# Attention scores of two cross attentions: one bf16 product of 100 rows becomes two float32r products in the row halves of the array

## What is computed

```python
q = split_heads(x @ Wq) / 4            # 2 x 16 heads x 256 x 16
k = split_heads(ctx @ Wk)              # 2 x 16 heads x 4096 x 16
v = split_heads(ctx @ Wv)
scores = einsum('bhqd,bhkd->bhqk', q, k)        # 256 x 4096 for each head
scores = where(mask, -inf, scores)     # layer 1: a large negative number is added
out = einsum('bhqk,bhkd->bhqd', softmax(scores), v)
```

## Time and profile before

| | |
|---|---|
| median of 3 runs | 2161.07 us (2157.18 to 2162.24) |
| profiled execution, span and time | 2163.9 us |
| attention 0, steps under way | about 64 to 519 us |
| attention 1, steps under way | about 760 to 1205 us |
| TensorE busy over the span | 92% |
| VectorE, ScalarE busy | 64%, 52% |

### The profile page before, as it was taken

One profiled execution on the slowest core, in us unless ns is written; L12 is line 12 of the kernel. 1 busy time (PEld: TensorE's weight loads), 2 busy tenths in 40 slices (PEclk: granted clock), 3 DMA queues, 4 the chain that ended last, 5 costly groups with the idle time before them and its releaser, 6 DMA issues.

```text
span 2163.9 us, 36756 instructions
## 1 busy us (share of the span) xinstructions
PE 1995.1 (92%) x13543; PEld 1176.1 (54%) x13543; DVE 1388.0 (64%) x3351; ACT 1131.3 (52%) x2555; POOL 590.4 (27%) x898
## 2 busy tenths in 40 slices
PE   7999999998998799999999888999898799798998
PEld 4545554444465444555445455546646588564656
DVE  4676667785567577666778475442227898577473
ACT  3566666676354366666667461142235587264342
POOL 2322222212542122222220060000015266363241
PEclk9999999999998899999999998999899899999999
DMA  8555445570101655544643201353200333200110
GB/s 192 131 134 123 107 107 136 114 183 15 39 21 40 106 122 133 128 104 106 157 99 60 71 12 35 100 185 98 64 20 2 117 108 93 88 2 8 40 52 10
DMA packets 122835, 187.27 MB, mean 87 GB/s; under 512 B 22920, under 2 KB 70592, under 8 KB 122304
## 3 DMA queue, kind: packets, MB, share of 16 engines
q1 hardware_dynamic: 121568, 183.90, 33.9%
q10 hardware_dynamic: 1088, 1.02, 0.2%
HBM read 131.86 MB, written 2.13 MB: 62 GB/s over the span
## 4 chain that ended last, share of the span: by engine, by line
PE 75%; DVE 12%; ACT 5%; SPq 3%; issue 2%; DMA 2%; POOL 1%; ACTq 0%; DVEq 0%; POOLq 0%
PE PS L759 10%; PE PS L741 10%; PE PS L709 9%; PE PS L340 8%; PE PS L653 5%; PE PS L348 4%; PE PS L665 4%; SPq L781 3%; PE PS L1768 3%; PE PS L1793 3%; PE PS L2201 2%; PE PS L449 2%; PE PS L2143 2%; PE PS L497 2%; PE PS L476 2%
## 5 line engine op out<-in xcount | busy, mean ns | idle before, releaser
L840 DVE TENSOR_REDUCE WK<-PS 128x1 f32<-128x1024 f32 x512 | 609.2, 1220 | 260.8 <-PE PS L709 258.7
L950 ACT ACTIVATE WK<-PS 128x512 f32<-128x512 f32 x1024 | 541.9, 601 | 192.4 <-PE PS L741 186.6
L741 PE MATMUL PS<-WK 100*128 100x256 bf16 x2048 | 323.6, 275 | 6.3 <-ACT WK L950 5.3
L709 PE MATMUL PS<-WK 100*128 100x512 bf16 x1024 | 306.6, 383 | 17.6 <-DMA WK<-scratch_q 5.1
L741 PEld LDWEIGHTS PS<-WK 100*128 100x128 bf16 x2048 | 166.8, 98 | 215.5 <-ACT WK L950 75.2
L759 PE MATMUL PS<-WK 128*32 128x256 f32 x3072 | 207.1, 386 | 0.0
L548 ACT ACTIVATE WK<-PS,WK 128x256 f32<-128x256 f32 (+1 forms) x320 | 140.6, 451 | 74.0 <-DVE WK L516 44.8
L574 POOL TENSOR_TENSOR WK<-WK 128x128 f32<-128x128 f32 (+1 forms) x128 | 64.9, 507 | 342.6 <-DVE WK L534 307.6
L1018 POOL TENSOR_SCALAR WK<-WK 128x2 bf16<-128x2 f32 x64 | 12.5, 195 | 527.5 <-DVE WK L846 329.8
L974 POOL TENSOR_TENSOR WK<-WK 128x512 f32<-128x512 f32 x62 | 71.7, 1157 | 256.9 <-ACT WK L924 147.9
L759 PEld LDWEIGHTS PS<-WK 128*32 128x32 f32 x3072 | 80.6, 109 | 112.4 <-issue 77.6
(11 more groups left out here) (340 smaller groups left out, 3247.7 us busy)
## 6 DMA issues: line engine op xcount, KB each, us to landing
WK<-WK SPq DMA_DIRECT2D x762, 64.0 KB
WB<-in_ctxT SPq DMA_DIRECT2D x78, 512.0 KB, 4.8
WK<-in_ctxT SPq DMA_DIRECT2D x40, 512.0 KB, 3.8
WA<-in_ctxT SPq DMA_DIRECT2D x26, 512.0 KB, 4.8
WK<-in_ctx SPq DMA_DIRECT2D x8, 1024.0 KB, 5.7
WK<-in_ctx SPq DMA_DIRECT2D x16, 512.0 KB, 4.2
WK<-scratch_q SPq DMA_DIRECT2D x24, 128.0 KB, 5.2
WB<-in_L3f_qkv SPq DMA_DIRECT2D x2, 1536.0 KB, 6.5
```

What stands on the lines that cost most here:

```text
L709: x = pe.e.matmul(b.ap[:, u, :], QS[0:100, h, bb * 256 + q * 128:bb * 256 + (q + 1) * 128], KS[s % 4][0:100, c * 1024 + u * 512:c * 1024 + ...
L741: x = pe.e.matmul(b.ap[:, j * 256:j * 256 + 256], KS[s % 4][0:100, kt * 128:(kt + 1) * 128], QS[0:100, h, bb * 256:bb * 256 + 256], start= ...
L840: dv.e.tensor_reduce(mt[:, n:n + 1], tile["R", L, s, n].rearrange("p a b -> p (a b)"), AX, ALU.max).then_inc(*dv.at("R", L, s, n))
L950: ac.e.activation(PR[n % NPR], tile["S", L, s, i], ACT.Exp).then_inc(*ac.at("E", L, s, i))
```

## The change

Instead of three pieces of bf16, a float32 number is split into two pieces of float32r (`FR`, 4 bytes, high and low). A score needs high times high, high times low and low times high: three blocks of 16 rows, two rows for the maxima and one for the mask, 51 rows in all. The two halves of a key tile lie below each other: keys 0 to 2047 on partitions 0 to 50, keys 2048 to 4095 on partitions 64 to 114, and the queries stand on both. `HALF[u]` picks one. A product of the first half uses the upper 64 rows of the array, one of the second the lower 64.

The order is written in **units** `U`, eight to a step: two `S` banks (2 by 2 products, halves alternating), then one `R` pair (one product from each half). `S` order 0 to 15 now alternates between the halves. The projections and `F` stand behind whole units. Before, an `R` stood behind the first `S` of a pair, and at the start of a step ahead of all `S`.

```diff
-        for i in range(16):
-            if i:
-                yield "S", s, i
-            if i % 2 == 0:
-                n = 4 + i // 2 if i < 8 else i // 2 - 4
-                if s + (1 if i < 8 else 2) < 32:
-                    yield "R", s + (1 if i < 8 else 2), n
-            if i == 0:
-                yield "S", s, 0
+        for i in range(0, 16, 2):
+            n = 4 + i // 2 if i < 8 else i // 2 - 4
+            r = s + (1 if i < 8 else 2)
+            row = (r, n) if r < 32 else None
+            yield "U", s, i, row
+            yield "S", s, i
+            if row:
+                yield "R", r, n
+            yield "S", s, i + 1
             if i == 2 and s:
                 if s + 1 < 24:
                     yield "L", s + 1
                 yield "F", s - 1, 3
                 yield "E0", s - 1
-            if i == 5 and 8 <= s < 16:
+            if i == 4 and 8 <= s < 16:
                 yield "V", 1, s - 8, s
             if i in (6, 10, 14):
                 yield "F", s, i // 4 - 1
-            if i == 9 and s < 24:
+            if i == 8 and s < 24:
                 yield "K", s // 4 + 2, s % 4
             if i == 14:
                 yield "M", s + 1
...
+            def row_half(s, n, u):
+
+                g, hh, bb, h = where(s)
+                q, c = n // 4, n % 4
+                return pe.e.matmul(tile["R", L, s, n][:, u, :], QS[HALF[u], g % 2, hh, q * 128:(q + 1) * 128],
+                                   KS[s % 4][HALF[u], c * 512:(c + 1) * 512], start=True, stop=True)
...
+            def column(s, i, j):
+
+                g, hh, bb, h = where(s)
+                kt = i // 2 * 2 + j
+                return pe.e.matmul(tile["S", L, s, i][:, j * 256:j * 256 + 256], KS[s % 4][HALF[i % 2], kt * 128:(kt + 1) * 128],
+                                   QS[HALF[i % 2], g % 2, hh, :], start=True, stop=True)
...
+                elif o[0] == "U":
+                    _, s, i, row = o
                     for u in range(2):
...
+                        column_bank(s, i + u)
+                    for j in range(2):
+                        for u in range(2):
+                            x = column(s, i + u, j)
+                            if j:
+                                x.then_inc(*pe.at("S", L, s, i + u))
+                    if row:
+                        row_bank(*row)
+                        row_half(*row, 0)
```

```diff
-                            pe.e.transpose(b.ap[:, 0, :].bitcast(BF)[96:99, q * 128:(q + 1) * 128], nb[:, q, 0:3],
-                                           idb[:, :]).then_inc(*pe.at("M", L, s, q))
+                            pe.e.transpose(b.ap[0:98, 0, q * 128:(q + 1) * 128], nbw[:, s % 2, q, :],
...
+            def column_bank(s, i):
+
+                settle(take(sr, ("S", L, s, i), (ac, "E", L, s, i)))
+                pe.wait_ge(dv, "M", L, s)
+                pe.wait_ge(ac, "MC", L, s)
+
...
+                elif o[0] == "M" and o[1] < 32:
+                    s = o[1]
+                    g, hh, bb, h = where(s)
+                    ac.wait_ge(pe, "M", L, s, 1)
+                    ac.e.activation(QS[96:98, g % 2, hh, :], tile["M", L, s][96:98, 0, 0:256], ACT.Copy).then_inc(
+                        *ac.at("MC", L, s))
```

More of the change, by code:

```diff
@@ L8 @@
 BF = mybir.dt.bfloat16
+FR = mybir.dt.float32r
 I32 = mybir.dt.int32
@@ L17 @@
 WKN = 34432
+QS0 = 29728
 class Signal:
@@ L594, in build @@
         RC = WK[:, 34352:34368].rearrange("p (q h) -> p q h", q=2)
[L595 to L598, removed]
+        mx, mxr = WK[:, 34368:34384], WK[:, 34384:34392]
+        q32 = view(WK, 20752, 1024, 2, 512)
+        qp = [view(WK, 21776 + 1024 * i, 1024, 2, 512) for i in range(2)]
         CT = [[view(WB, 6416, 1024, 2, 512), view(WB, 7440, 1024, 2, 512)] + more for more in (
@@ L601, in build @@
             [view(WA, 0, 1024, 2, 512), view(WA, 1024, 1024, 2, 512)])]
-        FT = [view(WK, 28192 + 1024 * i, 1024, 2, 512) for i in range(4)]
+        FT = [view(WK, a, 1024, 2, 512) for a in (26144, 27168, 28192, 25120)]
         vbuf = (0, 2, 0, 1)
@@ L1033, in xattn_pool, with query_rows, load_q @@
                     vconst(L, 1)
+                elif o[0] == "S" and o[1] in (8, 16) and o[2] == 2:
+                    po.wait_ge(pe, "S", L, o[1] - 1, 15)
+                    zero_rows(L, o[1] // 8 + 1)
         def key_rows(steps):
+            ones = onesf[0:2, :].rearrange("p (a b) -> p a b", a=1).to_broadcast([2, 16, 128])
             for s in steps:
-                sp.e.dma_start(WK[96:99, 2048 * s:2048 * s + 2048], D["c_krows"]).then_inc(*d_krows.at())
+                for u in range(2):
+                    sp.e.dma_start(KSW[s][64 * u + 32:64 * u + 34, :].rearrange("p (a b) -> p a b", a=16), ones).then_inc(
+                        *d_krows.at())
+        def query_rows(L):
+            ones = onesf[0:1, :].rearrange("p (a b) -> p a b", a=1).to_broadcast([1, 32, 128])
+            for u in range(2):
+                sp.e.dma_start(QSW[64 * u + 34:64 * u + 35, :].rearrange("p (a b) -> p a b", a=32), ones).then_inc(
+                    *d_qrows.at())
+            d_qrows.mark(L)
+        def load_q(L, g):
+            bb, m = g // 2, g % 2
+            for row, i in ((0, 0), (16, 0), (35, 1)):
+                for u in range(2):
+                    sp.e.dma_start(
+                        QSW[64 * u + row:64 * u + row + 16, m * 2048:m * 2048 + 2048].rearrange("p (h t) -> p h t", h=8),
+                        scrq[i][m * 128:(m + 1) * 128, bb * 256:(bb + 1) * 256].rearrange("(h p) t -> p h t", p=16)).then_inc(
+                        *d_qs[m].at())
+            d_qs[m].mark(L, g)
         def stack(L, s):
@@ L1074, in xattn_sp @@
                     sp.wait_ge(dv, "qp", L, m)
-                    for i in range(3):
+                    for i in range(2):
                         sp.e.dma_start(scrq[i][m * 128:(m + 1) * 128, :], qp[i][:, m, :]).then_inc(*d_qw[m].at())
```

205 lines of the change are left out of this document (89 added, 116 removed).

## The result

The changed kernel takes 2187.51 us (median; 2183.0 to 2190.01), the kernel before 2161.65 beside it (2157.18 to 2171.22). The ratio is 1.0112, 95% interval 1.0085 to 1.014: slower by 1.1%. Forecast were 2127 us and a chance of 0.65 for faster. The measured time lies in the stated range, on the other side of no change, where rival 4 stood. The profiled execution took 2183.0 us, with a span of 2181.6. It was the fastest of the four, so its trace shows 18 us of loss (2163.9 before), where the medians are 26 apart.

A forecast was written before the change was run, and what follows sets the result against it. TensorE's own work was taken as the bound. 16 plain steps at +0.10 us, 32 with `K` at -0.41, 16 with both at -0.92 and starts -8 gave -34, so 2127 us; range 2078 to 2203, the forecast's own 2096 to 2158.

The forecast's parts named there:

- rival 4: Handshakes cost more than counted (load 0.12 or above, seam over 1 us): 2158 to 2200 us; chance 0.10.
- rivals 1 and 2: TensorE: two-cycle columns or halves not overlapping, some 2310 us, chance 0.12; loads of the halves serial, some 2240, chance 0.06.
- The loop through the exponential: From a cycle's first `S` load through the exponential to the next load: 1.15 us, with TensorE standing for 0.66.
- The seam: Between steps, behind the last `F`: turns of the maxima, their copies and waits, 0.94 us where it was 0.44.
- rival 3: TensorE's gaps let its clock fall in the attentions: 2195 us; chance 0.04.
- A projection: `K` or `V` products behind a first unit: 0.66 us of each hidden in TensorE's wait, 0.51 gained by each.
- rival 5: Handshakes cost less and VectorE becomes the bound, floor 10.6 us a step; halfway there 2085 us; chance 0.08.
- The new cycle: Two units and `F`, four times a plain step: 1.15 + 0.49 + 1.10 = 2.74 us, against 2.84.
- The load that shows behind a wait: First pair's weight load after a wait: 0.06 us exposed, ends 0 and 0.12, worth 31 us either way.
- The way back from the exponential's end to the next load: In the loop, from the exponential's end to TensorE's next load: 0.06 us.
- From the last `R` to `F`: At a cycle's end: 0.21 us for the `R` pair, then `F` unchanged at 1.10.
- The rest: Splits, DMAs, `zero_rows` and `load_q` give nothing; the attentions' starts and attention 0's first `R` give -8 us.

The follow-up runs named there:

- x6: Changed kernel with `R` ahead of the four `S` products only in the second unit of each pair: 2141.94 us, ratio 0.9906.
- x12: Changed kernel with the exponential on only the first 256 of a bank's 512 columns (output differs): 2131.0 us, ratio 0.9856.
- x2: Changed kernel with each `S` bank waited for and filled alone, in the old order (`S`, `R`, `S`): 2126.19 us, ratio 0.9844.
- x3: Changed kernel with `R` ahead of the four `S` products in every unit: 2159.8 us, ratio 0.9995.
- x4: Changed kernel with four pairs of `F`'s products behind every unit instead of eight behind every second: 2184.62 us, ratio 1.0105.
- x1: Kernel before, bf16 products kept, issued in the changed kernel's units (wait for both banks, then `S`, `S`, `R`): 2228.22 us, ratio 1.0305.
- x10: x7 with the turns of the maxima ahead of the step's third `F`: 2126.62 us, ratio 0.9845.
- x7: Changed kernel with each `S` bank waited for alone and `R`'s product of one half beside the other half's two `S`: 2126.95 us, ratio 0.9831.

## Why the prediction was wrong

What held. Float32r takes a column a cycle, and the halves run together: rivals 1 and 2 did not come. The Trainium skill (FP8 and Floating Point Precision, TensorE Precision Notes) sets a reduced FP32 beside a true FP32 of four passes, and gives the reduced one no count. The single pass was the prediction's inference; `S` at 0.51 for four bears it out. The loop through the exponential is where TensorE stands: 1.25 less a unit's own 0.13 + 0.22 + 0.21 is 0.69, where 0.66 was foretold. The seam is 0.89 (0.94). The clock stayed near full (rival 3). A projection adds what it was costed at: `K` 1.39 (1.44), `V` 3.20 (3.04). VectorE didn't become the bound (rival 5).

The step that failed is **The new cycle**, 1.15 + 0.49 + 1.10 = 2.74, which measured 1.25 + 0.69 + 1.00 = 2.94. The mechanism was right and its sizes were short, term by term:

- The load that shows behind a wait: 0.06 taken, 0.13 measured (from a unit's load to its `R` 0.35, less the 0.22 of two pairs). It enters a cycle twice. In the second unit it adds 0.07. In the loop it adds 0.05: from the load to the exponential 0.54 pass (1156.91 to 1157.45), where 0.49 was taken. I halved the 0.12 of the float32 row-part products because the passes are half; the load is not a pass, and the row-part row itself was the right price. The Trainium skill (TensorE: Matmul & The Clock Gate, Weight-path perf modes and LDWEIGHTS) leads to some 107 ns for such a load, as an estimate. What shows, 0.13, is near it; the load's own record is longer, 0.186.
- The way back from the exponential's end to the next load: 0.06 taken from VectorE's release of an `R` bank, 0.11 measured (1157.45 + 0.60 to 1158.16). This adds 0.05.
- From the last `R` to `F`: 0.34 from the start of `R`, where 0.21 was taken for `R` and 0.10 stood in `F`'s 1.10. This adds 0.03.
- Together 0.07 + 0.05 + 0.05 + 0.03 = 0.20, by which the cycle is off.

0.20 x 256 = 51 us, 0.80 a step: with it the three steps forecast come to 12.70, 14.14 and 17.18, and 12.65, 14.04 (attention 1) and 17.24 were measured. The second failure is **The rest**: 8 us from the starts. The first `R` of attention 0 starts 1.2 us sooner (38.66, 39.84), the first copy 0.3. Attention 1's first `R` comes 218.8 us behind attention 0's last copy instead of 222.7, and its first copy then 21.2 us later instead of 18.0: it loses most of it again. Its timeline, and two stretches around it:

```profile
748.97 1.22 PE L664 MATMUL PS<-KSR,QSR 51*128 51x512 f32 x4 [3.20 <-DMA QSR<-scratch_q]
```

```profile
744.00:754.00 10.00, 6.80 (x22) 1.88 (x22) 2.35 (x2) 2.26 (x5) 1.26 (x1) 0.72 1.18 143
754.00:764.00 10.00, 8.20 (x24) 2.43 (x26) 6.46 (x6) 2.02 (x4) 2.53 (x2) 0.50 0.98 120
```

The clock there is 0.72 and then 0.50; the second stretch is wholly at TensorE's lower level, 1.2 GHz. In the same two stretches of the kernel before (736.7 to 756.7) it was 0.66 and then 1.00. In all, 2127 + 51 + 8 = 2186, and 2187.5 was measured. That this closes so well is partly luck: between the profiled executions the steps lost 19 us where the forecast had a gain of 26, which is 45 and not 51. Some steps with `K` of the kernel before took 14.8 to 15.0 instead of 13.75, and the sum knows nothing of them.

So the outcome is rival 4, "load 0.12 or above", which had 0.10. The error was in the weights. The sum rested on the difference of two numbers near 2.8, each made of some ten terms, and one that had no row of its own (0, 0.06 or 0.12) moved the result by 31 us either way, as much as the whole gain. The upper end was a measured row and the value taken was not. Four places off in the same direction by 0.03 to 0.07 turned the sign. That the range held the time is owed to the bounds, not to the value.

What the forecast did not ask is where `R` should stand. It put both `R` of a cycle behind the `S` and let the wait be empty; moving one of them ahead of the wait, in x6, was worth 46 us.

What stays open: why x12's steps with `K` gain as much as 0.77; what holds x2 and its neighbours at 2126; what the two banks at once cost the bf16 kernel without the move of `R`; and whether a fourth `S` bank would let the pairs pay. All eight banks are taken, so no run has one.

## What to carry to other kernels

An edit that makes TensorE's products cheaper is worth nothing in a stretch where a buffer loop (product, reader, release) ends later than the products do; here that is the first unit of each cycle. Write down that loop before the sum, count how many buffers a new unit needs at once, and list what stands behind the product that waits. Here two of three banks at a time, with `R` behind them, cost 3.1%, more than half-price products earned (1.9%). In such a loop order is the cheap lever. What stands ahead of the product that starts the loop lengthens it; the same work behind it, or ahead of the product that waits, is free (x3 against x6, 18 us). Take the price of a term from the nearest row, and if you take less, say what for: here 0.06 instead of 0.12 was worth 31 us. And cost every kind of step by itself: long cover that looks wasteful in a plain step can be what hides the work of the others (x4).

## What the runs showed of the hardware

- Float32r products of 51 rows in the two row halves: four with 256 columns in 0.51 us, two with 512 in 0.40, against 0.61 and 0.59 for bf16 one after the other.
- A 4-byte weight load of 128 columns lasts 0.186 us and shows by 0.13 behind a wait; a bf16 load lasts 0.098 and shows by 0.02 (x1).
- The halves also run side by side with different work in each, two products of 256 columns beside one of 512. From the first load of these three to `F` pass 0.43 (x10, 1119.85 to 1120.28), and a unit of six takes 0.57 (x7). x2 takes 0.57 as well, though it issues its `S` products one bank after the other.
- VectorE's copy of 2x256 from float32 to float32r takes 0.42 us, where the bf16 copy of 3x256 took 0.30, three rows against two notwithstanding.
